# Turning h and z with VectorE block transposes and DMA in place of TensorE, with a new order of work on each engine

## The reference, cut to what matters

```python
def block(h, p):                                  # once per layer
    r = _retention(h, wk)                         # causal, rows divided by max(|row sum|, 1)
    a, gate = jnp.split(r @ w1 + b1, 2, axis=-1)
    m = a * jax.nn.silu(gate) @ w2 + b2
    m = _groupnorm1(m, gg, gb)                    # one mean and variance per sequence
    y = m + h
    f = jax.nn.gelu(y @ wf1 + bf1_, approximate=False) @ wf2 + bf2_
    return (_layernorm(f + y, lg, lb), None)      # mean and variance per token
```

## Time and profile before

| what | us |
|---|---|
| median of 3 runs (2429.24 to 2431.05) | 2429.43 |
| the profiled execution | 2427.29 |
| its span, first to last instruction | 2425.6 |
| TensorE (PE) busy | 2398.8 |
| DVE busy | 1548.2 |
| ACT busy | 1367.1 |
| POOL busy | 1356.7 |

### The profile page before, as it was taken

How to read it: one execution, slowest core, us unless ns; L and a number is a source line. 1 busy time by engine, 2 the same in 40 slices (tenths; PEclk the granted TensorE clock), 3 DMA queues, 4 the chain that set the end, 5 groups by cost and what they waited for, 6 DMA issues and landing times. The chain is left out here.

```text
span 2425.6 us, 35215 instructions
## 1 busy us (share of the span) xinstructions
PE 2398.8 (99%) x11674; PEld 2007.9 (83%) x11674; DVE 1548.2 (64%) x2877; ACT 1367.1 (56%) x2403; POOL 1356.7 (56%) x1255
## 2 busy tenths in 40 slices
PE   9999999999999999999999999999999999999998
PEld 7888888888888888878888888888888888888886
DVE  4666666666666666778787856665646656564445
ACT  5666766667666666666655544444444444444443
POOL 2355655455544644567888955545545546554444
PEclk9999999999999999999999999999999999999999
DMA  7011121111100112127665564544445443444442
GB/s 252 27 52 43 36 79 35 35 35 46 58 26 17 36 44 70 35 89 233 238 208 191 181 224 145 185 149 160 149 161 186 159 153 145 154 151 169 152 161 74
DMA packets 106822, 287.64 MB, mean 119 GB/s; under 512 B 7360, under 2 KB 77248, under 8 KB 90304
## 3 DMA queue, kind: packets, MB, share of 16 engines
q1 hardware_dynamic: 105856, 285.16, 34.2%
q10 hardware_dynamic: 832, 0.82, 0.1%
HBM read 216.36 MB, written 69.60 MB: 118 GB/s over the span
## 5 line engine op out<-in xcount | busy, mean ns | idle before, releaser
L711 POOL TENSOR_TENSOR hid_lo<-full,hid_hi 128x512 fp32r<-128x512 f32 x384 | 504.8, 1329 | 514.9 <-ACT full L1015 462.7
L1520 DVE SCALAR_TENSOR_TENSOR full<-ps,bias_cols,sum 128x512 f32<-128x512 f32 x384 | 288.2, 750 | 218.2 <-PE ps L1799 198.6
L1797 PE MATMUL ps<-hid_hi,m_w 128*128 128x512 f32 x1024 | 401.8, 392 | 0.1
L1799 PE MATMUL ps<-hid_hi,m_w 128*128 128x512 f32 x1024 | 398.8, 389 | 0.0
L1798 PE MATMUL ps<-hid_lo,m_w 128*128 128x512 f32 x1024 | 398.5, 389 | 0.0
L1012 ACT ACTIVATE hid_hi<-ps,bias_cols 128x512 fp32r<-128x512 f32 x128 | 88.3, 690 | 496.6 <-PE ps L1799 496.6
L1797 PE MATMUL ps<-te_hi,m_w 128*128 128x512 f32 x896 | 351.1, 392 | 1.6 <-DVE sum L1507 0.9
L1799 PE MATMUL ps<-te_hi,m_w 128*128 128x512 f32 x896 | 348.9, 389 | 0.0
L1798 PE MATMUL ps<-te_lo,m_w 128*128 128x512 f32 x896 | 348.6, 389 | 0.0
L1799 PEld LDWEIGHTS ps<-hid_hi,m_w 128*128 128x128 f32 x1024 | 192.2, 188 | 40.5
L1797 PEld LDWEIGHTS ps<-hid_hi,m_w 128*128 128x128 f32 x1024 | 192.3, 188 | 39.5 <-issue 0.5
(11 more groups left out here) (212 smaller groups left out, 5586.0 us busy)
## 6 DMA issues: line engine op xcount, KB each, us to landing
m_w<-prepared SPq DMA_DIRECT2D x96, 1408.0 KB, 6.0
prepared<-m_w SPq DMA_DIRECT2D x32, 1408.0 KB, 5.8
h_store<-h_out SPq DMA_DIRECT2D x32, 512.0 KB, 3.2
we_raw<-in_W SPq DMA_DIRECT2D x64, 256.0 KB, 6.4
gate_bc<-gate_rows SPq DMA_DIRECT2D x64, 256.0 KB, 6.4
h_in<-h_store SPq DMA_DIRECT2D x24, 512.0 KB, 4.4
h_in<-in_x SPq DMA_DIRECT2D x8, 512.0 KB, 5.9
raw<-in_Wf SPq DMA_DIRECT2D x8, 512.0 KB, 8.4
```

Source lines behind the costliest of these rows:

```text
L711: nc.gpsimd.tensor_tensor(out=hid_lo[:, k, :], in0=full[:, k, :], in1=f32(hid_hi[:, k, :]), op=ALU.subtract).then_inc(hid_ready, 1)
L1520: nc.vector.scalar_tensor_tensor(out=full[:, k, :], in0=src, scalar=b1_col(e, 2 * fp + BLOCK_ROW[k]), in1=other[:, :], op0=ALU.add, op1=AL ...
L1797: nc.tensor.matmul(out, w[0], x[0], start=first, stop=False, skip_group_check=True)
L1799: return nc.tensor.matmul(out, w[1], x[0], start=False, stop=last, skip_group_check=True)
```

## The change

No h and no z (but the very last z of each slot) is turned on TensorE any more. `turn_z` transposes the 32x32 blocks of z (two 128x512 instructions on DVE), four DMAs of 32 partitions each (`store_z`) write the blocks to DRAM at their turned place, in runs of 32 floats, and one DMA (`load_z`) brings z back with tokens on partitions. `turn_h` does the same with h, in one 128x1024 instruction and four DMAs (`store_hT`), in 12 of the 16 steps; hT is loaded from DRAM to `hT_in` in every step (two DMAs). The layer's columns `lc` come by DMA, not by a DVE copy. The orders change: TensorE does `project_t(B)` ahead of `out_projection(A)`, and `group_moments(A)` after three quarters of `down_projection(B, 1)`; the last two blocks of `scores` wait for `residual` (the DVE instruction that makes z out of banks 0 and 1); `residual(B, 1)` moves into A's `groupnorm_out`; B's layernorm runs a step later, its `layernorm_out` standing right behind `rstd_group(A)` on POOL; and `high_hT(B)` stands ahead of `hidden(B)` on ACT.

```diff
+    z_v = z_store.rearrange("s (k p) d -> s p k d", p=P)
+    hT_v = hT_store.rearrange("i s (c p) n -> i s p c n", p=P)
+    hT_blocks = hT_store.rearrange("i s (q b) (k r a) -> i s r b k q a", a=BLOCK, b=BLOCK, k=TB)
+    z_blocks = z_store.rearrange("s (n a) (c q b) -> s q a c n b", a=BLOCK, b=BLOCK, c=DC)
...
+        def turned_z(s):
+            return tmp[s][:, 0:DC, :]
...
+            def store_hT(s, it):
+                sp.wait_ge(h_turned, it * SLOTS + s + 1)
+                for r in range(P // BLOCK):
+                    sp.dma_start(hT_blocks[it + PAIRS, s, r],
+                                 z[s][r * BLOCK:(r + 1) * BLOCK, :, :].rearrange("p k (q a) -> p k q a", a=BLOCK)
+                                 ).then_inc(hT_stored[s], DMA)
+            def store_z(s, it):
+                sp.wait_ge(z_ready[s], it * U + U)
+                for q in range(P // BLOCK):
+                    sp.dma_start(z_blocks[s, q], turned_z(s)[q * BLOCK:(q + 1) * BLOCK, :, :].rearrange("p c (n b) -> p c n b", b=BLOCK)
+                                 ).then_inc(z_moved[s], DMA)
+            def load_z(s, it, turned=True):
+                sp.wait_ge(z_moved[s], it * Z_MOVE + Z_MOVE + Z_STORE)
+                if turned:
+                    sp.wait_ge(hT_stored[s], it * H_STORE + H_STORE)
+                sp.wait_ge(h_new[s], it * U + U)
+                sp.dma_start(z[s][:, :, :], z_v[s]).then_inc(z_moved[s], DMA)
+            def step(it, load, load_T, lc_of=None, lnv_a=None, lnv_b=None, earlier=True, turn=True):
+                store_z(A_, it - 1)
+                if lc_of is not None:
+                    load_lc(A_, lc_of)
+                if earlier and turn:
+                    store_hT(A_, it - 2)
+                load_z(A_, it - 1, turn)
+                load(A_, it + 1)
+                load_T(A_, it + 1)
+                if earlier:
+                    store_h(B_, it - 2)
+                if lnv_b is not None:
+                    load_lnv(B_, lnv_b)
+                store_z(B_, it - 1)
+                if lc_of is not None:
+                    load_lc(B_, lc_of)
+                load_T(B_, it + 1)
+                if earlier and turn:
+                    store_hT(B_, it - 2)
+                load_z(B_, it - 1, turn)
+                load(B_, it + 1)
+                store_h(A_, it - 1)
+                if lnv_a is not None:
+                    load_lnv(A_, lnv_a)
...
                 if seam:
                     split_weight("qk", now.layer)
-                if earlier:
-                    layernorm_out(pool, nc.gpsimd, B_, earlier)
                 split_h(A_, now)
...
                     split_h(B_, now)
-                if before:
                     split_f(B_, before)
+                    if earlier:
+                        layernorm_rstd(B_, earlier)
                     layernorm_rstd(A_, before)
...
                 if seam:
-                    for name in ("f1", "f2"):
-                        split_weight(name, now.layer)
+                    split_weight("f1", now.layer)
                 rstd_group(A_, now)
+                if seam:
+                    split_weight("f2", now.layer)
+                if earlier:
+                    layernorm_out(pool, nc.gpsimd, B_, earlier)
                 if last:
                     sum_weights(0)
                 mask_scores(B_, now, range(TB))
...
                 if before:
-                    layernorm_rstd(B_, before)
                     layernorm_out(pool, nc.gpsimd, A_, before)
...
                     high_r(A_, now)
+                    high_hT(B_, now)
                     hidden(B_, before)
...
                 load_table(ACT.Gelu)
+                high_t(B_, now)
+                if before:
+                    normalise_z(A_, before)
+                else:
+                    act.wait_ge(fold_stored, (L - 1) * DMA)
+                if earlier:
+                    normalise_z(B_, earlier)
                 if seam:
                     next_high_weight("f2", now.layer, f2_psum[B_], before)
-                high_t(B_, now)
-                if before:
-                    keep_z(B_, before)
-                else:
-                    act.wait_ge(fold_stored, (L - 1) * DMA)
-                high_p(B_, now, (0,))
+                high_p(B_, now, (0, 1))
                 high_y(A_, now, 0)
-                high_p(B_, now, (1,))
+                high_p(B_, now, (2, 3))
                 high_y(A_, now, 1)
-                high_p(B_, now, (2, 3))
-                if before:
-                    normalise_z(A_, before)
+                if not last:
+                    high_hT(A_, step_behind(act, now))
                 hidden(A_, now)
...
-            def groupnorm_out(s, at, meanwhile=lambda part: None):
+            def groupnorm_out(s, at, meanwhile=lambda part: None, between=lambda: None):
...
                 summed(0)
+                between()
                 gained(1)
                 meanwhile(0)
                 low_y(s, at, 0)
...
+            def turn_z(s, at, c):
+                dve.wait_ge(z_ready[s], at.base + residuals(s, c))
+                nc.vector.transpose(turned_z(s)[:, c, :], y[s][:, c, :]).then_inc(z_ready[s], 1)
+            def turn_h(s, at):
+                dve.wait_ge(h_new[s], at.base + 2 * U)
+                nc.vector.transpose(z[s][:, :, :].rearrange("p k d -> p (k d)"),
+                                    h_out[s][:, :, :].rearrange("p k d -> p (k d)")).then_inc(h_turned, 1)
...
-            def body(now, before, seam, last=False, entry=False):
+            def body(now, before, earlier, seam, last=False, turn=True):
                 if before:
                     for c in range(DC):
                         residual(A_, before, c)
-                if seam:
-                    dve.wait_ge(z_ready[A_], before.base + U)
-                    hold(dve, held)
-                    next_constants(A_, now.layer)
-                if before:
-                    low_hT(A_, now, entry)
+                    for c in range(DC):
+                        turn_z(A_, before, c)
+                    if earlier and turn:
+                        turn_h(A_, earlier)
                     gated_products(B_, before)
...
                 low_r(A_, now)
+                low_hT(B_, now)
...
+                if earlier:
+                    for blocks in HALVES:
+                        layernorm_stats(B_, earlier, blocks)
+                    layernorm_var(B_, earlier)
                 if before:
                     gated_products(A_, now, lambda part: layernorm_stats(A_, before, HALVES[part]))
                     layernorm_var(A_, before)
                     residual(B_, before, 0)
+                    turn_z(B_, before, 0)
                 else:
-                    low_hT(B_, now, entry)
                     gated_products(A_, now)
+                for c in range(DC):
+                    low_t(B_, now, c)
+                groupnorm_in(A_, now)
+                groupnorm_var(A_, now)
+                groupnorm_out(A_, now, between=lambda: before and residual(B_, before, 1))
                 if before:
-                    low_hT(B_, now, entry)
-                groupnorm_in(A_, now)
-                if before:
-                    residual(B_, before, 1)
-                if seam:
-                    dve.wait_ge(z_ready[B_], before.base + U)
-                    hold(dve, held)
-                    next_constants(B_, now.layer)
-                low_t(B_, now, 0)
-                groupnorm_var(A_, now)
-                low_t(B_, now, 1)
-                groupnorm_out(A_, now)
+                    turn_z(B_, before, 1)
                 low_p(B_, now, range(TB))
-                if before:
-                    for blocks in HALVES:
-                        layernorm_stats(B_, before, blocks)
-                    layernorm_var(B_, before)
+                if not last:
+                    low_hT(A_, step_behind(dve, now))
+                if earlier and turn:
+                    turn_h(B_, earlier)
...
-            def scores(s, at, blocks):
+            def score(s, at, b, k, before):
+                q = slice(LO[b], S)
+                if k == 0 and b >= 2 and before:
+                    pe.wait_ge(z_ready[s], before.base + residuals(s, b - 2))
+                pe.wait_ge(t_lo[s], at.base + 2 * k + 2)
...
-            def body(now, before, seam, last=False, entry=False):
-                if not entry:
-                    transpose_h(A_, now)
+            def body(now, before, earlier, seam, last=False, turn=True):
                 if before:
                     gated_projection(B_, before)
                 for c in range(DC):
                     project_t(A_, now, c)
                 if before:
-                    transpose_z(A_, before)
                     out_projection(B_, before)
...
+                gated_projection(A_, now)
+                if before:
                     down_projection(B_, before, 0)
...
```

(61 more changed lines are left out.)

252 lines of the change are left out of this document (115 added, 137 removed).

## The result

The changed kernel takes 2491.1 us in the median (2487.8 to 2492.6), the kernel before 2429.5: ratio 1.025 (95% interval 1.0233 to 1.0268), slower by 62 us. Its profiled execution has a span of 2490.9. The forecast was 2476, slower, range 2385 to 2505.

A forecast was written before the change was run, and what follows sets the result against it. TensorE, 99% busy, bounds the kernel. Nine plain steps +33.3, steps 2 and 3 +9.2, seams +7.6 and step 1 -1.6 make +48.5 on 2427.3: 2476 us, range 2385 to 2505.

The forecast's parts named there:

- What is removed and added: 432 TensorE transpose instructions go, winning at most 48 us; DVE transposes cost 0.7 and 1.1 us, 5 us a step.
- First half of a step: From A's down projection to gated_projection(A): starts at 25.3 us instead of 27.0, a gain of 1.7.
- plain steps: The nine ordinary repeating steps: 68.4 us each instead of 64.69, +3.7 each, +33.3 in all.
- The stop: In A's group norm, POOL's layernorm_out(B) makes DVE's small L1326 and L1329 stand still; summed(0) comes 4.5 us late.
- rival 2: ACT 1 to 2 us late, so POOL's layernorm_out stops less of DVE: step 65.0, 2431 us; chance 0.07.
- Waits and clock: TensorE's second half: moments wait 0.7 us, scores' last block 5.05, then the 1.2 GHz clock costs 1.6.
- The sum: Whole kernel: the changes of all steps together make +48.5 us, 2476 us.
- step 1: Near the kernel's start, with no earlier B for POOL's layernorm_out: only a gain, -1.6 us.
- steps 2 and 3: Early steps, 63.8 us before: 68.4 after, +4.6 each, +9.2 together.
- seam steps: Three steps where split_weight("f2") also precedes layernorm_out on POOL: 69.9 us each, +7.6 in all.
- Rival 1: POOL doesn't stop DVE's small group norm operations, or comes late: step 62.2, 2393 us; chance 0.28.
- Rival 3: DMAs of store_z and store_hT set the time: at 50 ns per 128-byte run +216 us, 2640; chance 0.08.

The follow-up runs named there:

- experiment 11: The changed kernel with only step 0 and the last step put back to the order of the kernel before: 2490.6 us, ratio 1.025.
- experiment 1: The changed kernel with POOL's two layernorm_out instructions for B cut in place from 128x1024 to 128x8 elements: 2423.7 us, ratio 0.998.
- experiment 9: The kernel of experiment 6 with B's store_hT, load_z and store_h ahead of the load of A's next hT on SP: 2429.6 us, ratio 1.0006.
- experiment 6: The changed kernel with B's layernorm_out at the head of POOL's next body, B's dependent DMAs and turn_h a step later: 2557.7 us, ratio 1.053.
- experiment 2: The changed kernel with POOL waiting, ahead of layernorm_out(B), until DVE's last gained of A's group norm is written: 2480.8 us, ratio 1.021.
- experiment 5: The changed kernel with layernorm_out(B) in place as eight instructions of 128x256 instead of two of 128x1024: 2455.1 us, ratio 1.011.
- experiment 12: The kernel of experiment 9 with step 0 in its old order and POOL's layernorm_out waiting for normalise_x1 in the last step: 2422.4 us, ratio 0.9978.

## Why the forecast was right, and by how much it was off

**What is removed and added.** One transpose of 128x512 is 0.70 (0.7 forecast), of 128x1024 1.22 (1.1). Right.

**First half of a step.** `gated_projection(A)` starts 25.3 to 25.6 us behind the step's start in the plain steps (25.3 forecast).

**The stop.** L1371 2.35, L1374 2.19, L424 starting with L1371, the free slot for L1372 in POOL's gap: as written. Both `normalise_z` end 1.0 us ahead of L751's end (0.85 forecast), so POOL never started late, and rival 2 didn't occur. The exclusive lock that the Trainium skill describes ("SBUF — State Buffer", section "SBUF: two separate sides") agrees with this: the small operations take 0.65 to 0.69 us beside quarter instructions and 2.2 to 2.35 beside whole ones, and `gained`, with only one of its large operands in SBUF, isn't stopped.

**Waits and clock.** Moments 0.3 (0.7 forecast), scores 4.4 (5.05), lower clock 1.57 (1.6): a step of 68.0 for 68.4.

**The sum.** Each step of the changed kernel less the same step of the kernel before, from the start of one step (`gated_projection(B)`, with the turn of h ahead of it where there is one) to the start of the next, with the forecast beside it:

| part | measured, us | forecast, us |
|---|---|---|
| up to the start of step 1 | +5.4 | 0 |
| step 1 | +0.1 | -1.6 |
| steps 2 and 3 | +8.9 | +9.2 |
| plain steps, the last one left out (8) | +29.6 | +29.6 |
| seam steps (3) | +8.5 | +7.6 |
| the last step | +9.0 | +3.7 |
| behind it, the expert part | +3.8 | 0 |
| all | +65.3 | +48.5 |

The repeating steps are right; almost all of the 17 us missing lies at the two ends, and these are the terms that were mis-sized. The sum had nothing for step 0, where `up_projection` waited 3.3 us for the high part of y (experiment 11 gives 2.9 back by that step's order). It took the last step for one of nine plain ones. There TensorE waits 0.8 and 1.2 us for `low_u` and 1.1 for the moments, then 4.6 for `residual` by the same stop, and last 2.4 us for `ry_sp`, because `normalise_x1` takes 8.5 us in place of 4.5 beside POOL. The expert part, which the sum called untouched, begins at a granted clock of 0.50 behind that last wait; the rest of its 3.8 us was not followed.

At the seams the size was right by another way than forecast, which is luck. `split_weight("f2")`, ahead of `layernorm_out`, lets the small operations through (0.23 and 0.16 us). The two `summed` (2.21 and 2.87) and a `low_y` (1.54) are stopped in their place, and TensorE waits 1.7 us at the scores and 2.7 in `up_projection`.

**Rival 1** is what experiments 1 and 9 show: a step of 63.3, not 62.2. What I hadn't seen is `down_projection(A, 0)`: 3.76 us in experiment 1 for 2.74 before, with waits of 0.2 to 0.3 for POOL's `split_f`. POOL, then ACT, in experiment 1:

```profile
703.43 3.01 POOL L744 TENSOR_SCALAR_AFFINE_SELECT pf_sp<-pf_sp 128x128 fp32r<-128x128 f32 x8 [7.09 <-DVE pf_sp L1261]
706.41 3.80 POOL L728 TENSOR_TENSOR pf_sp<-tmp,pf_sp 128x512 fp32r<-128x512 f32 x3
```
```profile
703.11 1.39 ACT L992 ACTIVATE tmp<-ps,lc 128x512 f32<-128x512 f32 x2 [0.80 <-PE ps L1864]
```

`split_f` (L728) starts the moment the masks (L744) end, so the masks hold it up. They wait for DVE's `low_p`, now behind a transpose of 0.70, and take 3.0 us where the kernel before needs 2.0. ACT's `high_hT` for the next A, which now stands ahead of `hidden(A)`, isn't the cause: ACT then waited 0.8 us for TensorE. In the changed kernel `down_projection(A, 0)` takes 2.72, as before: the stop gives POOL the time. So the stop costs 4.7 us of step and not 5.8, the wait and the clock. That moving the masks or `low_p` would bring the 1 us back wasn't tried. So had rival 1 held, 2393 would still have been about 30 us too fast (experiment 1: 2424): without the stop the change is worth 1.4 us a plain step, not 2.45, and its ends cost some of that.

**Rival 3.** A store in small runs takes 1.1 us longer from issue to landing, all of it hidden: z of A, B's z and both turned h are never what DVE or TensorE wait for in the changed kernel. What is left of this rival is experiment 6: not the runs, but SP's order can make z late. The Trainium skill ("DMA: Bandwidth & Descriptors", section "Why small descriptors are slow (HBM only)") gives each packet a fixed overhead; that is borne out in direction (3.3 us for 2.2), and not as a bound of this kernel. The read-modify-write below 512 bytes that the prediction names stands in the "Specifications" of that page, not in the section it cites; no run here shows how much of the 1.1 us is due to it.

## What to carry to other kernels

Before moving a long two-input operation of GpSimd, list what VectorE does in those microseconds: here even operations on 128x2 elements waited for the end of GpSimd's current instruction, and if a chain of small ones sets TensorE's next start, each can lose a whole instruction. Idle time of GpSimd is no sign of a good place. Where the work can't be moved, cut it into short instructions; where it can, move with it every DMA that depends on it, and look at what the queue's earlier entries wait for. A forecast made for the repeating step needs one look of its own at the first and the last step.

## What was not expected of the hardware

- The clock fell to 1.2 GHz behind single idle stretches of TensorE of 4.4 us, of 3.15 (experiment 2) and of 2.2 (experiment 5), where I had allowed for it only at the first. It didn't fall each time. The row of 1 us is behind a wait of 2.16 us in experiment 5, the two long ones are that step and its next:

```profile
653.50:654.50 1.00, 1.00 (x4) 0.81 (x3) 0.86 (x1) 0.05 (x1) 0.31 (x1) 0.50 0.00 0
```
```profile
645.57:711.34 65.77, 63.13 (x320) 53.66 (x321) 47.77 (x106) 41.19 (x75) 34.24 (x42) 0.97 0.43 100
711.34:776.41 65.07, 62.49 (x321) 52.25 (x321) 47.27 (x106) 41.18 (x75) 34.78 (x42) 1.00 0.41 97
```

  In experiment 5 the granted clock fell behind all five waits of 2.1 to 2.2 us, and behind one of nine of 1.6 to 1.7. In experiment 2 it fell behind ten of thirteen waits of 3.1 us and stayed at 1.00 behind three. So the length of the wait alone doesn't decide it. Where it fell, `up_projection(A)` took 1.4 to 1.7 us longer in the steps shown here; part of that came back behind it, so that the two steps above differ by 0.7.
- DVE can stop POOL as well: L424, which starts 0.2 us behind a `low_y` in experiment 2 (665.94 to 666.62, POOL from 666.15), takes 2.73 for 2.39.
- Eight VectorE instructions of 128x256 took 4.5 us with POOL's four long ones held back (experiment 12) and 12.9 beside them (experiment 9): 8.4 us more, for the 9.6 that the four take.
